# Second products of an expert trip, by slot in three half steps instead of one run of 24 matmuls

## What is computed

```
x = x + 0.5 * ffn(layernorm(x))
x = x + attn(layernorm(x))          # 16 heads of 8, bias from a table by distance
x = x + 0.5 * ffn(layernorm(x))

def ffn(x):                          # (its own weights, the same in both places)
    x = x + msa(layernorm(x) * w + b)                # 16 heads of 8, softmax
    h = gelu(einsum('td,edh->teh', z, w1))           # z: layernorm of x; 8 experts, 128 -> 512
    y = einsum('teh,ehd->ted', h, w2)                # 512 -> 128
    return x + y[argmax(z @ gate_w + gate_b)]        # each token takes one expert
```

## Time and profile before

| | us |
|---|---|
| median of 3 runs (2449.7 to 2457.5) | 2452.49 |
| the profiled execution | 2455.49 |
| its span | 2453.7 |
| TensorE busy | 2142.3 (87%) |
| VectorE busy | 1934.2 (79%) |
| ScalarE busy | 1909.3 (78%) |
| GpSimd busy | 771.6 (31%) |
| mean granted clock of TensorE | 0.928 |
| maxima on VectorE, L1414 | 1216 of 1217 ns |
| exps on ScalarE, L1301 | 3072 of 600 ns |
| gelus, L1384 | 102 of 596 ns |
| table loads under L1384 and L1301 | 57 of 1283 ns |
| copy of second products, L1398 | 34 of 491 ns |
| second products on TensorE, L1248 | 99.6 in 816 instructions |

### The profile page before, as it was taken

One profiled execution on the slowest core, in us unless ns is written; L12 is line 12 of the kernel. 1 busy time (PEld: TensorE's weight loads), 2 busy tenths in 40 slices (PEclk: granted clock), 3 DMA queues, 4 the chain that ended last, 5 costly groups with the idle time before them and its releaser, 6 DMA issues. The chain is left out here.

```text
span 2453.7 us, 59789 instructions
## 1 busy us (share of the span) xinstructions
PE 2142.3 (87%) x22882; PEld 767.4 (31%) x22882; DVE 1934.2 (79%) x3219; ACT 1909.3 (78%) x3561; POOL 771.6 (31%) x1167
## 2 busy tenths in 40 slices
PE   5898988889987999999899999899888888988935
PEld 1222222225421323542233233222222223532425
DVE  7988899885788896578888898899989997569210
ACT  1788798789877777788778778788979888878822
POOL 1343533330634622032442032022161232062153
PEclk7899799899989999999999899999999999989967
DMA  4234422135304334642442332111101103622525
GB/s 112 79 90 123 119 61 71 44 97 161 79 24 102 97 99 128 198 124 69 112 110 80 93 93 80 44 32 43 29 20 42 37 20 104 186 48 61 141 81 145
DMA packets 265568, 213.37 MB, mean 87 GB/s; under 512 B 64241, under 2 KB 219761, under 8 KB 265250
## 3 DMA queue, kind: packets, MB, share of 16 engines
q1 hardware_dynamic: 254018, 201.15, 29.5%
q0 software_dynamic: 11264, 8.40, 1.9%
HBM read 159.62 MB, written 59.77 MB: 89 GB/s over the span
## 5 line engine op out<-in xcount | busy, mean ns | idle before, releaser
L1301 ACT ACTIVATE probs<-psum 128x512 f32<-128x512 f32 x3072 | 1619.5, 600 | 302.0 <-PE psum L1068 184.0
L1414 DVE TENSOR_REDUCE maxes<-psum 128x2 f32<-128x1024 f32 x1216 | 1421.9, 1217 | 248.7 <-PE psum L1036 238.2
L1105 PE MATMUL psum<-probs,v_ones 128*9 128x256 f32 (+1 forms) x11520 | 990.0, 417 | 0.0
L1068 PE MATMUL psum<-q_staged,k_staged 27*128 27x512 f16 x3072 | 803.3, 404 | 50.5 <-DMA q_staged<-neg_max 19.8
L1036 PE MATMUL psum<-k_staged,q_staged 24*128 24x512 f16 x3072 | 628.3, 407 | 161.1 <-DVE maxes L1414 124.3
L1419 DVE CUSTOM_DVE_ANT_0 biased<-psum,strips 128x512 bf16<-128x512 f32 x640 | 408.9, 686 | 94.5 <-PE psum L1036 77.9
L1036 PEld LDWEIGHTS psum<-k_staged,q_staged 24*128 24x128 f16 x3072 | 145.4, 91 | 900.5 <-DVE maxes L1414 514.2
L1068 PEld LDWEIGHTS psum<-q_staged,k_staged 27*128 27x128 f16 x3072 | 221.2, 91 | 174.6 <-ACT probs L1301 80.2
L1105 PEld LDWEIGHTS psum<-probs,v_ones 128*9 128x9 f32 x11520 | 171.9, 89 | 330.2 <-issue 232.6
L817 POOL TENSOR_SCALAR max_rest<-max_turned 128x32 f32<-128x32 f32 x96 | 28.4, 296 | 657.9 <-DVE max_turned L1457 655.7
L815 POOL TENSOR_SCALAR max_rest<-max_turned,far_bias_rows 128x32 f32<-128x32 f32 x32 | 13.0, 406 | 353.6 <-DVE max_turned L1457 353.3
(11 more groups left out here) (167 smaller groups left out, 1278.0 us busy)
## 6 DMA issues: line engine op xcount, KB each, us to landing
m_w<-in_w SPq DMA_DIRECT2D x204, 256.0 KB
near<-bias_near SPq DMA_DIRECT2D x128, 160.0 KB
strips<-bias_strips SPq DMA_DIRECT2D x64, 288.0 KB, 3.2
k_staged<-k_parts SPq DMA_DIRECT2D x192, 48.0 KB
heads<-heads_t SPq DMA_DIRECT2D x384, 18.0 KB
m_y<-sorted_tokens SPq DMA_DIRECT2D x34, 192.0 KB
expert_out<-m_out SPq DMA_DIRECT2D x34, 192.0 KB, 3.2
q_staged<-q_parts SPq DMA_DIRECT2D x128, 48.0 KB
```

Source lines behind the costliest of these rows:

```text
L1068: mm_ = pe.matmul(bank[:, :], k.kst[p][rows_, kt * P:(kt + 1) * P], queries, start=True, stop=not biased_)
L1105: last = pe.matmul(heads_bank[32 * j:32 * j + VC, columns], k.v[:, batch_of(u) * KT + kt, u % QUADS * 4 + j, :], probs[:, step % 3 * 4 + j ...
L1301: act.activation(probs[:, step % 3 * 4 + e % 4, :], bank[:, :], ACT.Exp, scale=unscale[is_mid(u)]).then_inc(taken, 1)
L1414: dve.reduce_max(maxes[u % 2][:, half, 2 * i:2 * i + 2, t, chunk], slot, AX.X).then_inc(drained, 1)
```

## The change

`DOWN_AT` puts slot 0 of a trip's second products after half step 0 of the trip's step 2, slot 1 after half step 1, slot 2 after half step 0 of step 3. Each slot opens its own bank, and is copied by its own instruction of 128x128; slot 0 waits for the second weights and (on ScalarE) for the previous store. The store of a trip and the loads of second weights with it move from its step 3 to its step 4.

```diff
-DOWN_STEPS = {trip_step(*key) + 2: [key] for key in TRIP_KEYS}
+DOWN_AT = ((2, 0), (2, 1), (3, 0))
+DOWN_STEPS = {}
+for key in TRIP_KEYS:
+    for r, (since, i) in enumerate(DOWN_AT):
+        DOWN_STEPS[trip_step(*key) + since, i] = (*key, r)
...
-                sp.wait_ge(taken, seat[("m_down", *trip_key(done - 2))] + 1)
+                sp.wait_ge(taken, seat[("m_down", *trip_key(done - 2), SLOTS - 1)] + 1)
...
-        sp.wait_ge(taken, seat["m_down", n, b, trip] + 1)
+        sp.wait_ge(taken, seat["m_down", n, b, trip, SLOTS - 1] + 1)
...
-                if step == trip_step(n, b, trip) + 3:
+                if step == trip_step(n, b, trip) + 4:
                     store_tokens(sp, n, b, trip)
...
-    def pe_down(pe, n, b, trip):
-
-        bank, done = open_bank(pe, "m_down", n, b, trip), trip_index(n, b, trip)
-        pe.wait_ge(w2_in[done % 2], (done // 2 + 1) * SLOTS * 16)
-        for r in range(SLOTS):
-            pe.wait_ge(taken, seat["m_hidden", n, b, trip, r] + 1)
-            for q in range(4):
-                last = pe.matmul(bank[:, r * P:(r + 1) * P], hidden[r][:, q * P:(q + 1) * P], w2[done % 2][r][:, q, :],
-                                 start=q == 0, stop=q == 3)
+    def pe_down(pe, n, b, trip, r):
+
+        bank, done = open_bank(pe, "m_down", n, b, trip, r), trip_index(n, b, trip)
+        if r == 0:
+            pe.wait_ge(w2_in[done % 2], (done // 2 + 1) * SLOTS * 16)
+        pe.wait_ge(taken, seat["m_hidden", n, b, trip, r] + 1)
+        for q in range(4):
+            last = pe.matmul(bank[:, 0:C], hidden[r][:, q * P:(q + 1) * P], w2[done % 2][r][:, q, :],
+                             start=q == 0, stop=q == 3)
         last.then_inc(scored, 1)
...
-            if done:
+            if done and r == 0:
                 act.wait_ge(m_stored, done * 16)
-            act.activation(expert_out[:, :, :], bank[:, 0:SLOTS * C].rearrange("p (r c) -> p r c", r=SLOTS),
-                           ACT.Copy, scale=0.5).then_inc(taken, 1)
+            act.activation(expert_out[:, r, :], bank[:, 0:C], ACT.Copy, scale=0.5).then_inc(taken, 1)
```

More of the change, by code:

```diff
@@ L263, in taken_places @@
                 put("exp", u, e)
-        for n, b, trip in DOWN_STEPS.get(step, ()):
-            put("m_down", n, b, trip)
+        if (step, 0) in DOWN_STEPS:
+            put("m_down", *DOWN_STEPS[step, 0])
         if u < UNITS:
@@ L268, in taken_places @@
                 put("exp", u, e)
+        if (step, 1) in DOWN_STEPS:
+            put("m_down", *DOWN_STEPS[step, 1])
         for n, b, h in OUTPUTS:
@@ L1129, in pe_step @@
             pe_values(pe, u * UNIT_STEPS + t, i)
-            if i == 0:
-                pe_middle(pe, u * UNIT_STEPS + t)
+            pe_middle(pe, u * UNIT_STEPS + t, i)
     def pe_norms(pe, mid):
@@ L1239, in pe_hidden, with pe_middle @@
         last.then_inc(scored, 1)
-    def pe_down(pe, n, b, trip):
-        bank, done = open_bank(pe, "m_down", n, b, trip), trip_index(n, b, trip)
-        pe.wait_ge(w2_in[done % 2], (done // 2 + 1) * SLOTS * 16)
-        for r in range(SLOTS):
-            pe.wait_ge(taken, seat["m_hidden", n, b, trip, r] + 1)
-            for q in range(4):
-                last = pe.matmul(bank[:, r * P:(r + 1) * P], hidden[r][:, q * P:(q + 1) * P], w2[done % 2][r][:, q, :],
-                                 start=q == 0, stop=q == 3)
+    def pe_down(pe, n, b, trip, r):
[6 more added lines that the diff above has]
+                             start=q == 0, stop=q == 3)
         last.then_inc(scored, 1)
-    def pe_middle(pe, step):
-        for n, b, trip in DOWN_STEPS.get(step, ()):
-            pe_down(pe, n, b, trip)
+    def pe_middle(pe, step, i):
+        if (step, i) in DOWN_STEPS:
+            pe_down(pe, *DOWN_STEPS[step, i])
     def pe_between(pe, step):
@@ L1390, in act_scales, with act_middle @@
         act.reg_load(unscale[mid], scale_of[mid][0:1, 3:4].bitcast(I32))
-    def act_middle(act, step):
-        for n, b, trip in DOWN_STEPS.get(step, ()):
-            bank, done = take(act, "m_down", n, b, trip), trip_index(n, b, trip)
-            if done:
+    def act_middle(act, step, i):
+        if (step, i) in DOWN_STEPS:
+            n, b, trip, r = DOWN_STEPS[step, i]
+            bank, done = take(act, "m_down", n, b, trip, r), trip_index(n, b, trip)
+            if done and r == 0:
                 act.wait_ge(m_stored, done * 16)
-            act.activation(expert_out[:, :, :], bank[:, 0:SLOTS * C].rearrange("p (r c) -> p r c", r=SLOTS),
-                           ACT.Copy, scale=0.5).then_inc(taken, 1)
+            act.activation(expert_out[:, r, :], bank[:, 0:C], ACT.Copy, scale=0.5).then_inc(taken, 1)
     def dve_max(dve, u, m):
@@ L1823, in _ @@
                         act_heads(act, step // KT - 1)
-                    if i == 0:
-                        act_middle(act, step)
+                    act_middle(act, step, i)
                 act_between(act, step)
@@ L1851, in _ @@
                         pe_values(pe, step, i)
-                        if i == 0:
-                            pe_middle(pe, step)
+                        pe_middle(pe, step, i)
                 pe_between(pe, step)
```

## The result

The changed kernel takes 2484.31 us (median of 4 runs, 2474.43 to 2494.7), the kernel before 2453.88 (4 runs). The ratio is 1.0126, 95% interval 1.0093 to 1.0159: **slower by 1.3%, where 1.3% and 2484 were forecast**. The four runs spread over 20 us, so that a forecast on the microsecond is in part luck; its parts have to be looked at one by one, and several were off, in both directions.

What follows compares the result with a forecast made beforehand. TensorE and ScalarE were taken to bind trips together. Terms 11.2 + 3.0 + 5.1 + 1.5 + 10.1 + 0.6 = 31.5 us gave 2484 us (+1.3%) against the median of 2452.49; range 2464 to 2503.

Steps and rivals of the forecast that it cites:

- (1): ScalarE's copy of 384 columns becomes three of 128: 0.57 us for 0.39, +0.18 us a trip.
- (2): Trips without a store wait: TensorE stands for banks, the table load hides one slot; +0.8 us each, 11.2 in all.
- (3): Trips under bias, where TensorE alone binds: only its wait for banks counts, +0.6 us each, 3.0 in all.
- (4): Slot 0's copy waits earlier for the previous store: trip 1 +1.7 us, trip 4 +0.5, each three times; 5.1 and 1.5.
- the +0.5 for the queue: Part of trip 1's +1.7 us: the store moves one step down SP's queue, past one load.
- (5): Trip 5's store falls behind the carry of the maxima on SP, so trip 6's first copy waits: 10.1 us in all.
- rival C: More waits than counted: trip 3 may wait for its store, TensorE's stands may cost clock; 2495 to 2510, chance 0.13.
- (6): Tail without exps: next turn waits for the first copy, +0.4 us, and 0.2 for the trip ending the exps; 0.6.
- Rival B: Slower by ordinary trips alone, the carry not delaying trip 6: 2476, or 2465 at its small end; chance 0.22.
- A: Faster: split runs let exps and copies go on beside the products, -15 us, 2437; chance 0.08.

Runs made afterwards that it cites:

- the late store: Kernel before with two buffers for expert_out, and the store and loads of second weights one step later on SP: 2457.22 us, ratio 1.0014.
- the repeated run: Kernel before with two buffers for expert_out and nothing else, timed again unchanged: 2445.21 us, ratio 0.9965.

## Why the prediction came out right, and where its parts did not

**(1) Copies.** 0.28 us each was forecast and 0.279 measured; the +0.18 a trip was 0.12 by itself.

**(2) Ordinary trips.** +0.99 on average for +0.8, and +1.10 in the trip worked through. The mechanism holds: the stand for banks behind d0 ends where the sum put it, and the run moved by a half step gives 1.57 for 1.5. Mis-sized was the slot on TensorE, 1.09 us and not 0.96, three times.

**(3) Under bias.** +0.6 forecast. From the starts of first products, trip 0 of the second set takes 14.21 for 13.56, +0.65, trip 5 16.39 for 16.25, and trip 2 14.40 for 13.01. The average of these three is +0.73.

**(4) Trips 1 and 4.** Forecast +1.7 and +0.5. Trip 1 measured +0.9, -1.3 and +0.5 in the three sets, trip 4 +0.6, +1.6 and -3.1. The step that failed is that I held the point where c0 falls due at its old distance from the turn on VectorE. Slot 2 of trip 0 (555.96 to 557.05) now stands behind that turn, so the distance is 9.91 us and not 8.84 (556.65 to 566.89 - 0.33), and the wait shrinks by what the engines lost. The store itself landed 10.24, 12.37 and 10.52 us after the turn, where it took 9.91, 13.17 and 10.37 before: the +0.5 for the queue was not there every time. I had said that the engines slip for trip 4 and not for trip 1.

**(5) The crossing.** Waits of 2.2, 5.1 and 2.2 us forecast, 1.55, 4.17 and 2.04 measured, at +1.9, +7.0 and +3.9 us a trip for 2.4, 5.3 and 2.4. The copies fell due 7.7, 8.1 and 7.7 us after the turn, as forecast. The waits were a little shorter, since the store landed sooner than trip 1's row had it (9.2, 12.3 and 9.7 us after the turn for 9.9, 13.2 and 9.9); the price of the later two was higher, and behind both TensorE's granted clock had fallen (0.66 from 2172 to 2177 in the third set). The second set by stretch (columns as above):

```profile
1066.00:1072.00 6.00, 2.60 (x20) 1.16 (x19) 1.51 (x6) 1.82 (x4) 0.00 (x0) 0.90 0.14 41
1072.00:1078.00 6.00, 5.73 (x32) 3.90 (x32) 1.23 (x1) 2.74 (x7) 0.00 (x0) 0.54 0.62 182
```

and on TensorE:

```profile
1072.27 2.07 PE L1254 MATMUL psum<-m_w,m_hidden 128*128 128x128 f32 x8 [3.51 <-ACT m_out L1405]
1074.27 0.61 PE L1043 MATMUL psum<-k_staged,q_staged 24*128 24x512 f16 x2
...
1075.79 1.99 PE L1254 MATMUL psum<-m_w,m_hidden 128*128 128x128 f32 x8
1077.72 0.39 PE L1043 MATMUL psum<-k_staged,q_staged 24*128 24x512 f16 x2
```

The granted clock is 0.54 from 1072 to 1078, behind a stand of 3.51 us, and a slot takes 2.00 us instead of 1.09. In the prediction this was an allowance under rival C without a row; such a row was there, for trip 1 of the second set waits 3.66 us and TensorE's half steps behind it are longer (0.52 was granted from 988 to 991.2). It should have been read.

**(6) The tail.** +1.1 us for +0.6: 32.94 us from the first to the last first products of the last set, 31.86 before.

**The sum.** By the starts of first products the first three sets, the fourth and the tail take 7.0, 12.6, 4.9, 4.6 and 1.1 us more, 30.2 in all. The spans of the two profiled executions differ by 24.4 us (their times by 26.3): the stretches between the sets came out 5.8 us shorter, although the forecast put the +0.8 and +0.6 of the trips 7 into them, and the head and the end of the span differ by 1.9 us each, in opposite directions. I do not know why the stretches were shorter. The trips of (2) and (3) that have a next start gave 17.2 us for 12.0, of which 3.1 are trip 3 of the second set alone with its wait; the crossing gave 12.8 for 10.1 and the tail 1.1 for 0.6; trips 1 and 4 gave -0.9 for 6.6. The total is as right as it is because these errors cancel, and that is luck; the two mechanisms stand on the runs, at 13 us for the slots and 14 to 18 for SP's order. (Rival B's lower figure, 2465, adds up to 2463: 24 - 5.1 - 14 x 0.6 over 2452.5.)

**The rivals.** A (split runs let the engines overlap) fell: ScalarE waits more. By the rule of the Trainium skill, Perfetto Trace Analysis, section Matmuls, on rotating groups through banks, the change should have gained; here the groups rotate through three banks that the scores rotate through already, and c1 and c2 wait 0.96 and 0.52 us all the same. B fell, since all three trips 6 wait. C was partly there: trip 3's wait of 1.91 us in one set, and the clock; the time stayed well below its 2495.

## What to carry to other kernels

A long run of one engine's work is not a bad neighbour by itself. If it stands exactly under a pause of the other engine (here a table load and the two exps behind it), cutting it in three and spreading the thirds moves two of them out from under the pause; look first for what covers the run. When an instruction is split, ask where its waits go: the wait for the store moved to the first third, ahead of work that used to be done by then, and the store moved a step down a queue, past a transfer that it had always led. And a second buffer for the output tile took 0.35 to 0.76% off every kernel in which it was tried, more than any order of the matmuls.

## What was not expected of the hardware

- A group of float32 matmul instructions of 128x128 costs 0.19 us once beside 0.112 us for each: 8, 16 and 24 take 1.09, 1.99 and 2.88 us until the matmuls of another kind behind them start.
- Behind stands of TensorE of 3.5 and 5.0 us the granted clock was 0.54 and 0.51 in the next stretch of 6 us, near the lower of the two levels, so that a wait cost more than its length: the 5.04 us before trip 7 with the late store made its copy wait 8.48 us, where it waited 0.89 in the repeated run. Shorter stands went both ways in the changed kernel: 0.57 behind one of 0.94 us (1019 to 1023) and 1.00 behind one of 2.29 us (1037.9 to 1042). The length of the last stand alone does not tell.
